# First stage of a fused two-layer cross-attention kernel: queue order, one sine per table, coefficients computed earlier, taps in eight batches, and two layer norms folded into weights

## The reference, cut to what matters

```python
def layernorm(x, g, b, eps=1e-05):
    m = x.mean(-1, keepdims=True); v = x.var(-1, keepdims=True)
    return (x - m) * jax.lax.rsqrt(v + eps) * g + b
def s4d(x, log_dt, A_re, A_im, C_re, C_im, D_skip):      # N_STATE = 64
    dt = jnp.exp(log_dt); A = A_re + 1j * A_im; C = C_re + 1j * C_im
    dtA = dt[:, None] * A
    dC = C * (jnp.exp(dtA) - 1.0) / A
    powers = jnp.exp(dtA[:, :, None] * jnp.arange(L))
    K = 2.0 * jnp.einsum('dn,dnl->dl', dC, powers).real
    ...                                                   # y = x convolved with K along the tokens
    return y + x * D_skip
K = x_vision @ Wk; V = x_vision @ Wv
...                                                       # top-32 attention gives c_t
x = layernorm(x_text, g_norm_in, b_norm_in)
scale_in, shift_in = jnp.split(c_t @ W_film_in + b_film_in, 2, axis=-1)
x = x * (1.0 + mod_gate * scale_in) + mod_gate * shift_in
y = s4d(x, log_dt, A_re, A_im, C_re, C_im, D_skip)
...                                                       # y scaled and shifted likewise
xt = x_text + y
h = layernorm(xt, g_ffn, b_ffn)
h = jax.nn.gelu(h @ W1 + b1, approximate=False) @ W2 + b2
```

## Time and profile before

| | us |
|---|---|
| median of 3 runs | 1897.56 (1893.65 to 1898.56) |
| the profiled execution | 1905.53 |
| its span, first to last instruction | 1903.7 |
| mean granted TensorE clock, share of full speed | 0.914 |
| first stage | 0 to 164 |
| top-32 attention of layer one | 164 to 807 |
| filter stage | 807 to 878 |
| both feed-forward parts of layer one, queries of layer two | 878 to 984 |
| attention and experts of layer two | 984 to 1904 |

### The profile page before, as it was taken

How to read it: one execution, slowest core, us unless ns; L and a number is a source line. 1 busy time by engine, 2 the same in 40 slices (tenths; PEclk the granted TensorE clock), 3 DMA queues, 4 the chain that set the end, 5 groups by cost and what they waited for, 6 DMA issues and landing times. The chain is left out here.

```text
span 1903.7 us, 22744 instructions
## 1 busy us (share of the span) xinstructions
PE 1593.5 (84%) x8253; PEld 607.4 (32%) x8253; DVE 860.2 (45%) x2332; ACT 1388.3 (73%) x1444; POOL 168.3 (9%) x154
## 2 busy tenths in 40 slices
PE   5468778988989985586679999999999999995997
PEld 3345334545545544543221111111111111113332
DVE  4665899999999998464330000000000000003323
ACT  5753778888788876312259999999999999992332
POOL 4650011011111111000000000000000000000000
PEclk9777989999999998688659999999999999997998
DMA  3430379688697797361000002200310000003000
GB/s 95 121 111 27 70 153 202 154 197 191 141 219 165 156 228 196 81 175 46 4 18 1 1 1 35 39 1 1 48 26 1 1 1 1 1 1 96 0 1 12
DMA packets 69264, 143.54 MB, mean 75 GB/s; under 512 B 21738, under 2 KB 40643, under 8 KB 68219
## 3 DMA queue, kind: packets, MB, share of 16 engines
q0 software_dynamic: 13616, 75.73, 19.9%
q1 hardware_dynamic: 55098, 65.43, 13.0%
q10 hardware_dynamic: 432, 0.85, 0.1%
HBM read 52.78 MB, written 13.99 MB: 35 GB/s over the span
## 5 line engine op out<-in xcount | busy, mean ns | idle before, releaser
L1926 ACT ACTIVATE ex<-ps 128x1536 f32<-128x1536 f32 x536 | 721.9, 1493 | 5.5 <-PE ps L1880 5.4
L855 PE MATMUL ps<-K,qst 128*128 128x512 f32 (+1 forms) x832 | 394.0, 605 | 35.8 <-ACT srow L925 23.4
L1895 PE MATMUL ps<-ex,V 128*9 128x512 f32 x3200 | 419.2, 596 | 0.5 <-ACT ex L1926 0.4
L1880 PE MATMUL ps<-Q,K 52*128 52x512 bf16 (+1 forms) x1632 | 322.7, 385 | 39.1 <-ACT ex L1926 34.2
L1936 DVE COPY o<-ps 9x512 f32<-9x512 f32 x32 | 22.0, 687 | 713.7 <-PE ps L1899 713.0
L1056 DVE MAX8 cand<-srow 128x8 f32<-128x200 f32 (+1 forms) x1024 | 319.0, 360 | 8.3 <-ACT srow L925 8.3
L1016 DVE SCALAR_TENSOR_TENSOR both<-srow,top,both 128x1536 f32<-128x1536 f32 (+1 forms) x128 | 239.5, 1871 | 24.6 <-ACT both L942 24.2
L925 ACT COPY srow<-ps 128x1024 f32<-128x1024 f32 (+1 forms) x224 | 205.1, 924 | 46.8 <-PE ps L855 46.1
L942 ACT ACTIVATE both<-srow,shift 128x1536 f32<-128x1536 f32 (+1 forms) x128 | 209.6, 1639 | 25.4 <-DMA both<-both 24.1
L855 PEld LDWEIGHTS ps<-K,qst 128*128 128x128 f32 x832 | 150.5, 198 | 172.7 <-issue 117.5
L1880 PEld LDWEIGHTS ps<-Q,K 52*128 52x128 bf16 (+1 forms) x1632 | 60.6, 94 | 447.7 <-ACT ex L1926 433.2
(11 more groups left out here) (327 smaller groups left out, 1114.7 us busy)
## 6 DMA issues: line engine op xcount, KB each, us to landing
both<-both POOLq DMA_DIRECT2D x69, 768.0 KB, 8.9
v_ring<-v_rows SPq DMA_DIRECT2D x84, 256.0 KB, 5.4
both<-both POOLq DMA_DIRECT2D x23, 898.0 KB, 13.1
K<-k_parts SPq DMA_DIRECT2D x48, 204.0 KB
k_parts<-kl SPq DMA_DIRECT2D x12, 384.0 KB, 2.6
V<-v_rows SPq DMA_DIRECT2D x4, 900.0 KB, 7.0
v_rows<-v1g SPq DMA_DIRECT2D x12, 288.0 KB, 3.8
srow<-v_rows SPq DMA_DIRECT2D x1, 3200.0 KB, 17.6
```

The lines of the kernel that those rows point to most:

```text
L855: last = M.matmul(ps[:, BANK_OF[item] + b, 0:c1 - c0], qst[:, h, :], K0[:, c0:c1], start=True, stop=True)
L1880: last = M.matmul(out, K1[rows_, quad % 2, hh // 2, keys], Q1[rows_, 4 * quad + hh, tb * TB:(tb + 1) * TB], start=True, stop=True, tile_po ...
L1895: last = M.matmul(out, V1[:, quad % 2, g, VW * j:VW * j + VW], ex1[:, slot(w, 4 * g + j), :], start=g == 0, stop=False, tile_position=(0, ...
L1926: C.activation(ex1[:, s:s + NBANK, :], ps[:, b:b + NBANK, :], ACT.Exp)\
```

## The change

- SyncE issues the load of group i ahead of `store(i - 3)`, no longer behind it.
- The phases get a quarter turn on rows 0 to 63 (`cos_turn`), so that one sine over all 128 rows gives cosine and sine together. Three sines of 128 rows take the place of six of 64; one of two absolute values goes. The second operation of `phases` is now a SCALAR_TENSOR_TENSOR, and the first has a scalar from memory.
- `s4_roots` and `s4_coefficients` stand ahead of group 0 on VectorE; the table pieces behind them move up.
- The taps are made in eight batches of 16 channels, each in a PSUM bank of its own in the order of `TAP_BANKS`. A batch waits only for what reads its bank.
- `g_norm_in` and `b_norm_in` are folded into the FiLM weights and biases, `g_ffn` and `b_ffn` into `W1` and `b1`. The square root moves ahead on ScalarE.
- `PE_AT` is given twice: the new line has `"coefficients": 2`, and the old one with 8 still stands below it, so that 8 holds.

```diff
-        DVE_AT = {"rates": 0, "b_turns": 1, "b_phases": 2, "a_turns": 3, "a_phases": 4, "roots": 5, "b_table": 6,
-                  "coefficients": 7, "a_real": 9, "a_imag": 10, "a_sum": 11, "a_table": 12}
+        DVE_AT = {"rates": 0, "b_turns": 1, "b_phases": 2, "a_turns": 3, "a_phases": 4, "b_table": 5,
+                  "a_real": 6, "a_imag": 8, "a_sum": 9, "a_table": 10}
+        PE_AT = {"rates": 0, "coefficients": 2}
+        TAP_BANKS = (3, 4, 1, 2, 5, 6, 7, 0)
         HALF_STEPS = KTAP // 2
         PE_AT = {"rates": 0, "coefficients": 8}
...
-                    C.activation(table_(work), table_(phase), ACT.Abs).then_inc(S("abs_done"), 1)
+                    C.activation(table_(zb), table_(phase), ACT.Sin, scale=-TURN, bias=cos_angle[:, 0:1]).then_inc(S("trig_done"), 1)
...
-                    ts(table_(scratch), table_(dst), ROUND, ROUND, ALU.add, ALU.subtract)
-                    V.tensor_tensor(table_(dst), table_(dst), table_(scratch), ALU.subtract).then_inc(S("phase_ready"), 1)
+                    ts(table_(scratch), table_(dst), cos_turn[:, 0:1], ROUND, ALU.add, ALU.add)
+                    V.scalar_tensor_tensor(table_(dst), table_(scratch), ROUND, table_(dst), ALU.subtract, ALU.subtract)\
+                        .then_inc(S("phase_ready"), 1)
...
+                s4_roots()
+                s4_coefficients()
...
-                pe.wait_ge(S("v0_evac"), NGROUP)
-                pe.wait_ge(S("v1_evac"), NGROUP)
-                pe.wait_ge(S("k0_evac"), NGROUP)
-                pe.wait_ge(S("k1_evac"), NGROUP)
...
+                for b, bank in enumerate(TAP_BANKS):
+                    if bank == v_banks(NGROUP - 2)[0]:
+                        pe.wait_ge(S("v0_evac"), NGROUP - 1)
+                        pe.wait_ge(S("v1_evac"), NGROUP - 1)
+                    if bank == 5:
+                        pe.wait_ge(S("k0_evac"), NGROUP)
+                        pe.wait_ge(S("k1_evac"), NGROUP)
...
+                for f in range(NF):
+                    last = M.matmul(ps[:, 6, f:f + 1], w1[:, f * P:(f + 1) * P], gbf[:, 1:2], start=True, stop=True)
...
-                dchain(V.tensor_tensor(w(xf), w(xf), every_tile(rowsb["g_norm_in"]), ALU.mult))
-                dchain(V.tensor_tensor(w(xf), w(xf), every_tile(rowsb["b_norm_in"]), ALU.add))
...
-                        V.tensor_tensor(xf[:, t - 1, :], xf[:, t - 1, :], film[:, t - 1, 0, :], ALU.mult).then_inc(S("xf_scaled"), 1)
+                        V.scalar_tensor_tensor(xf[:, t - 1, :], xn[:, t - 1, :], mv[:, t - 1, 0:1], film[:, t - 1, 0, :],
+                                               ALU.subtract, ALU.mult).then_inc(S("xf_scaled"), 1)
...
-                dchain(V.tensor_tensor(w(xf), w(xf), every_tile(rowsb["g_ffn"]), ALU.mult))
-                dchain(V.tensor_tensor(w(xf), w(xf), every_tile(rowsb["b_ffn"]), ALU.add))
```

More of the change, by code:

```diff
@@ L315, in _ @@
                                      .rearrange("(c p) d -> p c d", p=P)).then_inc(S(f"ctx_in{i % NR}"), 16)
+                    if i == STORE_LAG:
+                        sp.wait_ge(S("xn_ready"), NT)
+                        sp.dma_start(xn_rows, xn_first[:, :, :]).then_inc(S("xn_out"), 16)
+                    if i >= STORE_LAG:
+                        store(i - STORE_LAG)
                 for i in range(NGROUP - STORE_LAG, NGROUP):
@@ L363, in _ @@
                 table_ = lambda t: t[:, :, :]
[L365 to L374, removed]
                 def s4_mag(rate, first):
@@ L535, in s4_coefficients @@
                         ts(rows[:, 2, half], a(t1), sign, None, ALU.mult)
-                        ts(rows[:, 3, half], a(t2), -2.0, None, ALU.mult)
+                        ts(rows[:, 3, half], a(t2), sign, None, ALU.mult)
                     V.tensor_copy(dt[:, :], dt[:, :]).then_inc(S("rows_ready"), 1)
@@ L577, in s4_taps @@
                 def s4_taps():
[L580 to L581 removed]
+                    for b, bank in enumerate(TAP_BANKS):
+                        dve.wait_ge(S("taps_ps"), b + 1)
+                        src = ps[0:KTAP, bank, :].rearrange("p (d m r) -> p m d r", m=NT, r=4)
                         for r in range(4):
[L583 to L587 removed]
+                            V.tensor_copy(taps[KTAP * r:KTAP * (r + 1), :, b * TAPS_PER_BANK:(b + 1) * TAPS_PER_BANK],
+                                          src[:, :, :, r]).then_inc(S("taps_ready"), 1)
                     dve.wait_ge(S("taps_ready"), 32)
@@ L592, in _ @@
                 dchain(V.memset(ones[:, :], 1.0))
+                for tile, value in ((cos_turn, 0.25), (cos_angle, QUARTER)):
+                    V.memset(tile[0:NS, :], value).then_inc(S("cos_ready"), 1)
+                    V.memset(tile[NS:P, :], 0.0).then_inc(S("cos_ready"), 1)
                 dve.wait_ge(S("x_in"), 16)
@@ L697, in _ @@
                         last.then_inc(S("rowsT_ps"), 1)
-                pe.wait_ge(S("v0_evac"), NGROUP)
-                pe.wait_ge(S("v1_evac"), NGROUP)
-                pe.wait_ge(S("k0_evac"), NGROUP)
-                pe.wait_ge(S("k1_evac"), NGROUP)
                 pe.wait_ge(S("zb_ready"), 1)
                 pe.wait_ge(S("ua_ready"), 1)
-                for d in range(D):
-                    last = M.matmul(ps[0:KTAP, d // 16, (d % 16) * KTAP:(d % 16 + 1) * KTAP],
-                                    zb[:, :, d], ua[:, :, d], start=True, stop=True)
-                    if d % 64 == 63:
-                        last.then_inc(S("taps_ps"), 1)
+                for b, bank in enumerate(TAP_BANKS):
+                    if bank == v_banks(NGROUP - 2)[0]:
[4 more added lines that the diff above has]
+                        pe.wait_ge(S("k1_evac"), NGROUP)
+                    if bank == v_banks(NGROUP - 1)[0]:
+                        pe.wait_ge(S("v0_evac"), NGROUP)
+                        pe.wait_ge(S("v1_evac"), NGROUP)
+                    for n in range(TAPS_PER_BANK):
+                        d = b * TAPS_PER_BANK + n
+                        last = M.matmul(ps[0:KTAP, bank, n * KTAP:(n + 1) * KTAP], zb[:, :, d], ua[:, :, d], start=True, stop=True)
+                    last.then_inc(S("taps_ps"), 1)
     NI = H0 * NT
@@ L1331, in program @@
         bf = sb(b5, "bf", [P, HID])
-        rowsb = {n: sb(b5, "row_" + n, [P, D]) for n in ("g_norm_in", "b_norm_in", "g_ffn", "b_ffn")}
+        rowsb = {n: sb(b5, "row_" + n, [P, D]) for n in ("g_norm_in", "b_norm_in")}
+        gbf = sb(b5, "gbf", [P, 2])
+        fold = sb(b5, "fold", [P, 2, D])
         dft = sb(b5, "dft", [P, 9, P])
@@ L1415, in _ @@
                     last.then_inc(S("spec_x_ps"), 1)
+                pe.wait_ge(S("film_read"), NT)
+                pe.wait_ge(S("w1_in"), 16 * 4)
+                for f in range(NF):
+                    last = M.matmul(ps[:, 6, f:f + 1], w1[:, f * P:(f + 1) * P], gbf[:, 1:2], start=True, stop=True)
+                last.then_inc(S("b1_ps"), 1)
                 pe.wait_ge(S("spec_k_ready"), 2)
```

92 lines of the change are left out of this document (43 added, 49 removed).

## The result

| | before | after |
|---|---|---|
| median of 4 runs, us | 1898.06 (1893.65 to 1901.94) | 1854.23 (1853.19 to 1856.06) |
| the profiled execution, us | 1905.53 | 1853.31 |
| ratio, 95% interval | | 0.9771 (0.9747 to 0.9794) |

What follows compares the result with a forecast made beforehand. Waits bound the first stage, set by the ring of splits, stores and loads. First stage 30.2 plus filter stage 7.8 gave 38.0 us: 1905.53 to 1867.5 profiled, less 8.0 for the median, 1859.6 us; range 1848 to 1875.

Steps and rivals of the forecast that it cites:

- wait ahead of `rowsT`: First stage, VectorE behind group 6: a new wait of 11 us for transposes TensorE still has behind group 8.
- The ring: First stage before: a split lets off a load, and that load the split two groups later; 9.3 us a group.
- the unchanged ring: Rival, chance 0.13: groups keep 9.3 us, first stage ends at 158.4, 5.3 gained there; kernel takes 1884.5 us.
- the short wait: Rival, chance 0.11: splits slip in between passes, `rowsT` behind group 6 waits 3 instead of 11; kernel takes 1851.6 us.
- the slower case: Rival, chance 0.04: VectorE's queue turns into the ring's pace from group 6; first stage ends at 185.6, kernel 1911.7 us.
- the end of the split of group 4: First stage, GpSimd: this split, held by the two passes before, was to end near 70.6 us.
- the 4.8 us of waits in group 6: First stage, VectorE: `k1f` waits for a split held under two passes, `v1g` for a store's landing; 4.8 us together.
- the 87.2 for the transposes: First stage: time when TensorE's transposes behind group 8, for which `rowsT` waits, are done, with semaphores: 87.2 us.
- the work of 41.6: First stage, VectorE until the end of group 6: groups 12.3, rate rows 2.7, phases and big passes; 41.6 us without waits.
- Alone this is worth nothing: First stage, ScalarE loses 14.7 us of sines and absolute value, worth nothing alone because ScalarE has slack.
- The price of 2.7: First stage: with coefficients ahead of the groups, VectorE ends them at about 28.5, 2.7 us later than its first `kabs` before.
- the other bound, 828.7: Filter stage: the transform of x starts at 828.7 if GpSimd's sums hold nothing, 2.6 us faster than the 831.3 taken.

Runs made afterwards that it cites:

- e4: Kernel after with the second `PE_AT` line removed, so coefficient rows are turned behind group 2, not 8; median 1852.3 us, ratio 0.9764 to the kernel before.
- e9: Kernel before with only the new sines, phases and signs; median 1895.1 us, ratio 0.9991 (0.9970 to 1.0013).
- e7: Kernel after with the taps behind one wait for all groups and copied in two halves of 16; median 1866.7 us, ratio 0.9840 to the kernel before.
- e5: Kernel after with the coefficient pieces back inside the groups (roots behind group 4, coefficients behind 6); median 1861.7 us, ratio 0.9802 to the kernel before.
- e10: Kernel before with the new sines and SyncE's loads ahead of the stores; median 1883.1 us, ratio 0.9918.
- e11: Kernel after with GpSimd's two filter-stage sums held until the FiLM loop is done; median 1863.9 us, ratio 0.9816 to the kernel before.
- e3: Kernel before with the changed filter stage alone (norms folded into weights); median 1885.8 us, ratio 0.9944.

## Why the prediction was right, point by point

| step | forecast | measured |
|---|---|---|
| VectorE free for group 0 | 28.5 | 28.36 |
| VectorE ends group 6 | 76 | 71.9 |
| wait ahead of `rowsT` | 11 | 11.16 |
| from there until `ua` is ready | 26.3 | 26.1 |
| taps | 18.6 | 18.59 |
| behind the last pass | 1.4 | 1.6 |
| end of the first stage | 133.5 | 129.5 |
| start of the transform | 6.0 earlier | 6.1 |
| from the start of the transform to that of the way back, with the products for `b1` | 0.7 longer | 0.3 shorter |
| end of the filter stage | -2.5 | -2.7 |
| behind the filter stage | 0 | -3.3 |

**The mechanism was right.** The ring let go: VectorE, which before was busy 82.2 of 116 us, is now busy 40.2 of the 43.6 us until group 6, and the wait stands where it was forecast. The forgotten `PE_AT` costs 2.5 in the profile of e4 (3 forecast), which the times can't confirm. Of the rivals, the unchanged ring was refuted by the wait for `ctx_in`, the short wait by the 11.16, the slower case by the first stage itself.

**The mis-sized term is the end of the split of group 4.** I put it at 70.6, held under the two passes before it. Both the 4.8 us of waits in group 6 and the 87.2 for the transposes rest on this. In the trace the split was held under the pass over `phaseA` only; its last part slipped in at 64.77, ahead of the pass over `zb` at 65.84, and ended at 65.93, 4.7 earlier. From there the load (67.66) and the turn (71.57) followed as I had added them up, groups 7 and 8 took 11.1 instead of 10.1, and the copy of `rowsT` stood at 83.11, 4.1 before the 87.2. That is the 4 us by which the stage beat the forecast. It is what the rival of the short wait had said of splits, but for one split and not for all.

VectorE was early by as much: of the 43.6 us 3.4 were idle, and 1.4 of these are the gaps that the work of 41.6 had in it, so it waited 2 and not 6. `k1f` of group 6 (68.34, done at 69.0) was ready under the pass over `zb`, which ended at 70.3. Alone this would only have made the wait longer, since what ended the wait was TensorE. That the wait came out at 11.16 against 11 is luck, then: both of its ends moved by 4.1. There is luck in the 41.6 as well: the seven passes took 28.4 where I had 26.6, the rate rows 1.7 where I had 2.7.

**A wrong statement that cost nothing: the sines.** "Alone this is worth nothing" is not refuted by the time of e9, whose interval reaches to 5.7 us less, but the stage ended 5.7 earlier, and ScalarE's slack, read from its 89 us of work in 164, was no slack: its copies of the context stand in the ring. In the kernel after, doubling the sines costs 8.1 us of the stage. The share of busy time did not tell this; the wait of TensorE for `ctxT` does.

**The taps and the coefficients were right in place and low in price.** Letting the first batches go is worth some 9 (e7), most of it because of the store that group 12 waits for; the sum named the 2.8 that fewer copies behind the last batch save, and not the rest. The four copies took 1.22 where I had 0.9. The price of 2.7 for the coefficients ahead of the groups was right (2.8 by e5), but what it saves is more than their 15 us of before: 21.1 in the closer groups of e5, where the roots take twice as long beside the splits. Taken back one by one, the four parts cost 23.8 + 10.6 + 8.1 + 7.5 = 50.0 of a gain of 34.2; alone, the three that were tried give 17.5, 5.7 and 3.1. (e7 takes back 1.4 too much.) This fits the waits: where one part is missing, as the early coefficients in e10, that part is late next and hides what the others give. For the parts that were not tried in pairs it is not shown.

**The filter stage.** The start of the transform lies at 831.2 in the time of before, for which I took 831.3, and e11 gives 828.6 for the other bound, 828.7. So the rule of the Trainium skill (SBUF — State Buffer, section "Who interferes with whom") bites in this loop as well, and its price is 2.6 us. Putting GpSimd's sums behind the loop, as in e11, is dearer than bearing it. The stage gave 9.0 where the sum had 7.8: the four products for `b1` took 0.95, but the transform was 0.66 shorter (5.21 instead of 5.87), a wait of 0.25 behind it fell away, and the rows overlap by 0.3. What the sum lacked is the time behind the stage, 3.3 us in the profiles of before and after and 4.1 in e3: TensorE's granted clock in the kernel before, in the 10 and the 120 us from its first `W1` product:

```profile
881.00:891.00 10.00, 9.96 (x21) 0.74 0.01 2
891.00:1011.00 120.00, 83.75 (x336) 0.67 0.03 9
```

After it was 0.84 and 0.70, and in e3 the same. Over all fourteen profiles the rest goes with the clock of those 10 us: 1018.6 to 1019.9 us in the seven with 0.82 to 0.84, 1020.8 to 1022.7 in the six with 0.74 to 0.78, and 1024.2 in e11 with 0.72. The kernels with the old filter stage all lie in the middle group. But e7, with the filter code of the kernel after, lies there too and loses 3.0 us, so what decides the clock there stays open.

The median: 34.2 + 9.0 + 3.3 = 46.5 by the stages, 43.8 by the medians, 38.0 in the sum. The difference between the first two is within the spread of the second stage. That this stage changed its length, by 5.6 us, I had named as a sign of being wrong; over fourteen profiles it is spread, and the sign was badly chosen.

## What to carry to other kernels

In a queue that both loads and stores, put the load ahead of the store that waits: five moved lines alone gave half of what the first stage gained (17.5 of 34.2). An engine's busy share says nothing about slack when one of its short operations stands in a ring; look for who waits for it. When several queues are nearly as late as each other, price a part by taking it back from the changed kernel as well as by doing it alone: here the two differ by a factor of up to two and a half.

## What the runs showed of the hardware

- Small VectorE operations pay for GpSimd's in full: 21 of them took 5.3 us with GpSimd idle and 11.1 beside its splits, single ones 1.17 instead of 0.19.
- A short idle time of TensorE cost more than its length: after 4.08 us of waiting (e11) the same 72 passes took 26.29 us instead of 23.50, at a granted clock of 0.50, half of full speed, in the first 4.7 us, where the kernel after had 1.00. The rest of the program was 4.8 us longer in the same profile, at 0.72 and 0.64 where the kernel after had 0.84 and 0.70; that the wait did this too is not shown, for e7 is 3.0 longer there without such a wait.
- VectorE's pass with one tensor and a scalar per row read from memory costs as much as one with two constants: 2.34 us against 2.28 for 4096 columns. The SCALAR_TENSOR_TENSOR took 4.71 and 5.26, both beside a split; the operation on two tensors that it replaces took 4.71 beside one.
- A sine over 64 rows and one over 128 rows take the same 3.7 us.
